# One-hots of targets and ranks in the second layer: whole-group tensor_tensor comparisons replaced by one tensor_scalar per tile of 128 edges

## What is computed

```
h = relu(layernorm(x));  x = x + L0(h)      # gather h@W by src, scale, segment_sum by dst, gelu
h = relu(layernorm(x));  x = x + L1(h)
# L1, per edge:  relu(concat(h[src], h[dst], edge) @ msg_W1 + b1) @ msg_W2 + b2
#                agg = segment_sum(of these, dst)
#     per node:  relu(concat(agg, h) @ upd_W1 + b1) @ upd_W2 + b2
```

## Time and profile before

| what | value |
|---|---|
| median of 3 runs | 2360.42 us (2358.78 to 2361.4) |
| profiled execution: its time and its span | 2360.0 us and 2360.0 us |
| busy: PE, DVE, ACT, POOL | 91%, 72%, 48%, 70% of the span |
| message stage | from 866 to 2320 us |
| granted PE clock over that stage | 1.00 |

### The profile page before, as it was taken

The page is one execution under the profiler, slowest core; times in us unless marked ns, Lnnn a source line. Parts: engine busy times, 40 slices in busy tenths (PEclk is TensorE's granted clock), DMA queues, the critical chain, the costliest instruction groups (busy, mean ns, idle before and its releaser), DMA issues.

```text
span 2360.0 us, 72737 instructions
## 1 busy us (share of the span) xinstructions
PE 2148.9 (91%) x23689; PEld 1935.2 (82%) x23690; DVE 1690.4 (72%) x4590; ACT 1143.2 (48%) x2411; POOL 1654.0 (70%) x1577
## 2 busy tenths in 40 slices
PE   2255999999999759999999999999999999999998
PEld 1143788887888659999999999999999999999995
DVE  8866788887888676666666666666666666666663
ACT  0003888888888644444444444444444444444442
POOL 5476777777777126777777777777777777777771
PEclk7566999999999879999999999999999999999999
DMA  2001111111112033333333333333333333333332
GB/s 74 1 1 42 26 27 27 27 27 29 27 25 28 6 86 65 73 74 74 74 74 74 74 74 74 74 74 74 74 74 74 74 74 74 74 74 74 74 75 41
DMA packets 346918, 133.36 MB, mean 57 GB/s; under 512 B 305501, under 2 KB 322755, under 8 KB 346787
## 3 DMA queue, kind: packets, MB, share of 16 engines
q1 hardware_dynamic: 298980, 82.66, 15.6%
q0 software_dynamic: 47808, 49.05, 11.1%
HBM read 124.04 MB, written 7.52 MB: 56 GB/s over the span
## 4 chain that ended last, share of the span: by engine, by line
PE 86%; DVE 7%; issue 3%; POOL 2%; ACT 1%; DMA 1%; DVEq 0%; SPq 0%; PEld 0%; POOLq 0%; PEldq 0%; ACTq 0%
PE psum L1759 17%; PE psum L1701 14%; PE psum L1570 12%; PE psum L1773 12%; PE psum L1602 9%; PE psum L1692 8%; PE psum L1711 5%; PE psum L1591 2%; PE psum L1737 2%; POOL rows L684 2%; PE psum L1726 1%; PE psum L1581 1%; PE psum L1537 1%; DVE work L830 1%; PE psum L1831 1%
## 5 line engine op out<-in xcount | busy, mean ns | idle before, releaser
L684 POOL DMA_INDIRECT rows<-a_rows,idx x1078 | 1110.4, 1030 | 378.9 <-issue 369.5
L1339 ACT ACTIVATE hT<-psum 128x392 bf16<-128x392 f32 x1152 | 510.6, 501 | 105.3 <-PE psum L1602 98.2
L684 POOL DMA_INDIRECT rows<-g_rows,idx x416 | 430.9, 1036 | 149.1 <-issue 125.7
L1570 PE MATMUL psum<-work,hT 128*128 128x192 bf16 x3528 | 455.0, 246 | 0.3 <-ACT hT L1339 0.3
L1759 PE MATMUL psum<-edge_index,H 128*128 128x192 bf16 x4802 | 429.2, 246 | 1.8 <-DVE H L1109 1.7
L1392 ACT ACTIVATE eoT<-psum 128x512 f32<-128x512 f32 x392 | 213.7, 602 | 404.9 <-PE psum L1692 404.8
L1759 PEld LDWEIGHTS psum<-edge_index,H 128*128 128x128 bf16 x4802 | 398.3, 99 | 3.4 <-issue 1.9
L1570 PEld LDWEIGHTS psum<-work,hT 128*128 128x128 bf16 x3528 | 323.5, 99 | 70.7 <-issue 1.0
L1602 PE MATMUL psum<-Z,one_lo 128*128 128x392 f16 x1152 | 364.8, 338 | 17.0 <-DVE Z L946 16.8
L1701 PE MATMUL psum<-wb,eoT 128*128 128x64 f32 x3136 | 374.4, 273 | 0.0
L1701 PEld LDWEIGHTS psum<-wb,eoT 128*128 128x128 f32 x3136 | 365.6, 192 | 0.1
(11 more groups left out here) (272 smaller groups left out, 2012.6 us busy)
## 6 DMA issues: line engine op xcount, KB each, us to landing
work<-in_edge_attr_dram SPq DMA_DIRECT2D x392, 128.0 KB
rows<-a_rows,idx POOLq DMA_INDIRECT x1078
Z<-slot_code SPq DMA_DIRECT2D x98, 160.0 KB, 3.1
rows<-g_rows,idx POOLq DMA_INDIRECT x416
idx<-src_by_tile SPq DMA_DIRECT2D x200, 4.0 KB
wb<-b_rows SPq DMA_DIRECT2D x196, 16.0 KB
g_rows<-Y SPq DMA_DIRECT2D x1, 1600.0 KB, 8.9
a_rows<-Y SPq DMA_DIRECT2D x6, 256.0 KB, 2.6
```

What stands on the lines that cost most here:

```text
L684: pool.indirect_dma_start(out=rows[:, k, t, :], out_offset=None, in_=table, in_offset=bass.IndirectOffsetOnAxis(ap=idx[:, k, t:t + 1], axis=0)
L1339: nc.scalar.activation(counts[:, j % 2, :, t * SLOTS:(t + 1) * SLOTS], psum[:, t % 4, 0:KEYS].rearrange("p (h m) -> p h m", m=SLOTS), ACT.Copy
L1570: ins = TT.matmul(psum[:, 4 + (j + 1) % 2, 0:NPART * D], counts[:, (j + 1) % 2, h, :], gtab[:, h, :, :].rearrange("p k d -> p (k d)"), sta ...
```

## The change

In the message stage alone, the target one-hots of a superblock are made by 8 instructions of 64 columns, one a tile, each comparing the row of numbers `digit16` (fp16) with one f32 value per partition. In `edges_to_slots` the three tensor_tensor instructions of a group give way to 5 pairs of tensor_scalar, one pair a tile: 7 columns compared with `pe_bin` and multiplied by `pe_src` in one instruction, and 128 columns compared with `pe_slot`. The semaphore `bin_marked`, which stood between the comparison and the product, goes. `window_onehots` stays for the first layer.

```diff
                     def onehots_of(i, k):
                         dve.wait_ge(summed[1], r * NSB + i * U + k + 1)
-                        window_onehots(i * U + k, eo[:, k, :, D:2 * D]).then_inc(onehot[1], 1)
+                        for t in range(T):
+                            ins = V.tensor_scalar(eo[:, k, t, D:2 * D], digit16[:, 0:W], rel2[:, bass.ds((i * U + k) * T + t, 1)],
+                                                  None, ALU.is_equal)
+                        ins.then_inc(onehot[1], 1)
...
                         if not first:
                             dve.wait_ge(packed, n - 1)
-                        to_bin, to_rank = bin_src[:, g, 0:GTS[g], :], rank_oh[:, g, 0:GTS[g], :]
...
-                        V.tensor_tensor(to_bin, digits(BINS), each_edge(pe_bin, BINS), ALU.is_equal).then_inc(bin_marked, 1)
-                        V.tensor_tensor(to_rank, digits(P), each_edge(pe_slot, P), ALU.is_equal)
-                        dve.wait_ge(bin_marked, n + 1)
-                        V.tensor_tensor(to_bin, to_bin, each_edge(pe_src, BINS), ALU.mult).then_inc(ranked, 1)
+                        for t in range(GTS[g]):
+                            at = bass.ds(i * PT + GOFF[g] + t, 1)
+                            V.tensor_scalar(bin_src[:, g, t, :], digit16[:, 0:BINS], pe_bin[:, at], pe_src[:, at],
+                                            ALU.is_equal, ALU.mult)
+                            ins = V.tensor_scalar(rank_oh[:, g, t, :], digit16[:, 0:P], pe_slot[:, at], None, ALU.is_equal)
+                        ins.then_inc(ranked, 1)
```

More of the change, by code:

```diff
@@ L357, in gnn_two_layers @@
         code_in = [sem("code_in0"), sem("code_in1")]
-        bin_marked = sem("bin_marked")
         ranked = sem("ranked")
@@ L1081, in edges_to_slots @@
                         n = 2 * (r * NIT + i) + g
-                        tiles = bass.ds(i * PT + GOFF[g], GTS[g])
                         if not first:
                             dve.wait_ge(packed, n - 1)
-                        to_bin, to_rank = bin_src[:, g, 0:GTS[g], :], rank_oh[:, g, 0:GTS[g], :]
[L1087 to L1091, removed]
-                        V.tensor_tensor(to_bin, digits(BINS), each_edge(pe_bin, BINS), ALU.is_equal).then_inc(bin_marked, 1)
-                        V.tensor_tensor(to_rank, digits(P), each_edge(pe_slot, P), ALU.is_equal)
-                        dve.wait_ge(bin_marked, n + 1)
-                        V.tensor_tensor(to_bin, to_bin, each_edge(pe_src, BINS), ALU.mult).then_inc(ranked, 1)
+                        for t in range(GTS[g]):
[4 more added lines that the diff above has]
+                        ins.then_inc(ranked, 1)
                     def copy_packed(i, g):
```

## The result

The changed kernel takes 2476.72 us (median of 4 runs, 2474.82 to 2478.02), the kernel before 2359.61 beside it: a ratio of 1.0493, with a 95% interval of 1.0478 to 1.0507. That is 117 us more; 2482 was forecast, with 2385 to 2520 as its range. The profiled execution took 2478.02 us, and its span is 2476.2, which is 116.2 more than the span before.

The account below looks back on a forecast made before the run. PE, busy for 91% of the span, was taken as the bound, with DVE's ranked arriving just in time. 1.25 us later in 95 half turns is 119 us; 2360 + 119 + 3 = 2482 us, range 2385 to 2520.

Parts of the forecast that it names:

- The place: Ahead of L1726 in each half turn: PE's and DVE's chains, 1.63 and 1.53 us, arrive together, so DVE has no slack.
- The slack ahead of the third piece: DVE waits for PE before the third piece of rows, 0.36 us in the mean, which takes up part of the delay.
- Bins and ranks: Five pairs in edges_to_slots take 1.92 us instead of 1.02, 0.90 more, all ahead of ranked.
- The sum: ranked comes 0.35 + 0.90 = 1.25 us later in each of 95 half turns, 119 us in all.
- The odd step: The 0.71 us more for one-hots and the even step's leftover are covered by DVE's 3.11 us of idle time there.
- The rule of the Trainium skill: DVE's fixed cost is 60 ns: eight one-hots 0.75 us, five pairs 0.8 us, so the change would cost nothing.
- Cheaper pointers: Rival: short DVE instructions have 0.10 us fixed instead of 0.137 and 0.19; 22 us more, 2382 us; chance 0.16.
- free pointers: Rival: pointers on DVE cost nothing, 0.06 us fixed; PE could win at most 12 us, 2348 us; chance 0.03.
- columns at one a cycle: Rival: DVE columns cost 0.0012 us each, 2.3 us a half turn, 2580 us; chance 0.09 for over 2515.
- Hidden slack: Rival: PE's gap ahead of L1726 isn't the wait for ranked; over 1.3 us of unseen slack, 2360 us; chance 0.05.
- POOL: Rival: POOL's gathers set the pace; sparing them would win 88 us in 49 turns, 2272 us; chance 0.03.
- the gap of 0.13: PE's idle time ahead of L1726, 95 times, marked issue in the trace, read as the wait for ranked.

Follow-up runs that it names:

- the moved kernels: edges_to_slots moved from the even to the odd step, in the kernel before (2321.37 us) and in the changed kernel (2336.76 us).
- e1_onehots_alone: The kernel before with only the target one-hots made tile by tile, edges_to_slots as before: 2394.14 us, ratio 1.0140.
- e3_before_moved: The kernel before with edges_to_slots moved from the even to the odd step, two groups ahead instead of one: 2321.37 us, ratio 0.9836.

## Why the prediction was right

- **The place.** That DVE, at 68% of the stage, had no slack ahead of `ranked`, and that both chains from the end of L1773 arrive at L1726 together, was the step on which all rests. PE's 95 waits for L1090 show it, and the moved kernels confirm it. That the two chains arrive together was not quite so: DVE's was already the later one, by 0.39 us of PE's time. That made it safe to count all of the added delay.
- **The slack ahead of the third piece**, 0.36 us: right. `e1_onehots_alone` lost 34 us, against 0.70 x 95 = 67 without it.
- **One-hots**, 0.165 us each forecast, 0.163 measured: 1.31 against 1.32 for eight.
- **Bins and ranks**, 0.20 and 0.17 forecast, 0.19 and 0.16 measured; from first to last end 1.84 to 1.86 against 1.92. This is the term that was too large, by 0.07 us or 7 of the 119.
- **The sum.** A half turn is 1.22 us longer (15.93 against 14.71) where 1.25 was forecast. By its own terms with the measured prices it would be 0.05 less than that: 0.70 - 0.36 for the one-hots and 0.83 for the pairs are 1.17. The prediction had no term for the rest. The largest piece of it in the trace is DVE's pause between `add_sums` and the one-hots of the even step, 1.19 us in the mean instead of 1.12. So part of the closeness is luck: two small misses offset each other. Over the whole stage, from the third slot product to the last (95 half turns), the changed kernel takes 114.8 us more; the opening takes 2.3 more (2.5 was the estimate) and all that follows 0.9 less. That is the 116.2 between the spans.
- **The odd step**: covered, as said; DVE waits there for 2.6 to 2.9 us.
- **The rule of the Trainium skill** (VectorE: DVE Perf Modes, The TRN2 errata; 58 cycles, 60 ns fixed): the trace agrees for instructions with constants (0.07 us for 7 columns) and disagrees for those with pointers (0.16 and 0.19). The sum by these 58 cycles, no change, was wrong. The same section adds that the fixed term measured on a single instruction is about 150 cycles and not 58, which the prediction left out.
- **The rivals.** Cheaper pointers, free pointers and columns at one a cycle (0.21 and 0.29 us) are out by the prices. Hidden slack is out by PE's 95 waits, and a falling clock by the 1.00 over the stage. POOL did not set the pace; it idles now.
- **A reading that was wrong but did no harm**: the gap of 0.13 was taken for the whole of what PE loses by waiting in the kernel before. It loses 0.39, and the earlier trace rows, read as that gap, has 0.36 a time. The forecast used only the difference in `ranked`, so its sum was not touched; the rival that priced PE's possible gain at 12 us, and the expectation for `e3_before_moved`, were.

## What to carry to other kernels

Before pricing an edit on an engine with idle time, find where in its queue the idle time lies, and follow what leaves that queue last. Here 2.9 us of slack in one step were worth nothing to the step beside it, and moving the work one step earlier made the old instructions 39 us faster than before and the new ones 24. The price of a short instruction depends little on its columns (0.07 us with 7, 0.10 with 64 or 128, without a pointer), and each pointer that it reads raised it by 0.06. Here eight tensor_scalars took 1.31 us for the 0.61 of one tensor_tensor with 512 columns. To see what a wait costs PE, look at the weight loads too, and not only at the matmuls.

## What the runs showed of the hardware

- A pointer scalar costs DVE 0.06 us of start-to-start time, each, in instructions of 7 to 128 columns: 0.07, 0.19 with none and with two at 7 columns; 0.10 and 0.16 with none and with one at 64 and at 128.
- PE idle by its matmul records understates a wait for a semaphore by 0.26 to 0.27 us here, since the weight load that could have gone ahead is not seen there: 0.13 in the matmuls and 0.39 in the time, 1.34 and 1.61 in the changed kernel. The idle time of the weight loads (0.36 and 1.58) is within 0.03 of it.
- On three chips the same kernel took 3772 to 3818 us instead of 2360, with PE standing still between the matmuls of one group, a mean granted clock of 0.78 to 0.79 instead of 0.95, and nothing named as the cause. What that is stays open.
